# An attention block on one core: three Q or K products in one go, V behind the results, a written-out beginning and a new ending

## The reference

```
q, k, v = x @ Wq + bq, x @ Wk + bk, x @ Wv + bv          # 128x384 each, six heads of 64
s       = q_h @ k_h.T / sqrt(64) + where(adj, 0, -9e15)  # 128x128 for each head
p       = softmax(s)
ctx     = concat_h(p @ v_h)
y       = x + ctx @ Wf + bf
out     = (y - mean(y)) / sqrt(var(y) + 1e-5)
```

## Time and profile before

| what | value |
|---|---|
| median of three runs | 1030.92 us |
| the profiled execution's own time | 1031.09 us |
| its span, first to last instruction | 1029.3 us |
| TensorE busy | 1017.5 us, 99% |
| VectorE busy | 732.1 us, 71% |
| ScalarE busy | 596.4 us, 58% |
| GpSimd busy | 627.8 us, 61% |
| granted TensorE clock, mean | 0.999 |

### The profile page before, as it was taken

One profiled execution on the slowest core, in us unless ns is written; L12 is line 12 of the kernel. 1 busy time (PEld: TensorE's weight loads), 2 busy tenths in 40 slices (PEclk: granted clock), 3 DMA queues, 4 the chain that ended last, 5 costly groups with the idle time before them and its releaser, 6 DMA issues.

```text
span 1029.3 us, 26790 instructions
## 1 busy us (share of the span) xinstructions
PE 1017.5 (99%) x7185; PEld 906.5 (88%) x7185; DVE 732.1 (71%) x2822; ACT 596.4 (58%) x2127; POOL 627.8 (61%) x649
## 2 busy tenths in 40 slices
PE   8999999999999999999999999999999999999996
PEld 7889889889888898898888898888988988988886
DVE  3576777777677777767776776777777677767674
ACT  4565655656646656556556466465565565564563
POOL 1355666656665756656666566656566666666675
PEclk9999999999999999999999999999999999999999
DMA  7286676676666666766766766766667667666431
GB/s 197 77 209 183 174 192 159 177 193 164 181 183 168 189 177 171 195 166 173 193 161 175 192 162 185 186 166 190 172 172 196 165 176 184 166 176 183 146 122 62
DMA packets 337690, 176.48 MB, mean 171 GB/s; under 512 B 222336, under 2 KB 321792, under 8 KB 337664
## 3 DMA queue, kind: packets, MB, share of 16 engines
q1 hardware_dynamic: 336864, 175.79, 62.7%
q10 hardware_dynamic: 800, 0.39, 0.1%
HBM read 102.18 MB, written 73.92 MB: 171 GB/s over the span
## 4 chain that ended last, share of the span: by engine, by line
PE 98%; DVE 1%; issue 0%; ACT 0%; POOL 0%; POOLq 0%; DVEq 0%
PE qk_ps L379 14%; PE qk_ps L381 13%; PE qk_ps L380 13%; PE cov_ps L379 13%; PE cov_ps L381 13%; PE cov_ps L380 13%; PE scores_ps L395 9%; PE cov_ps L413 9%; PE qk_ps L475 0%; PE scores_ps L523 0%; DVE s_mask L606 0%; DVE xT_lo L595 0%; PE scores_ps L467 0%; PE scores_ps L483 0%; PE qk_ps L413 0%
## 5 line engine op out<-in xcount | busy, mean ns | idle before, releaser
L790 ACT ACTIVATE probs<-s_mask,neg_max 128x128 f32<-128x128 f32 x756 | 292.6, 390 | 4.3 <-DVE neg_max L612 4.3
L606 DVE CUSTOM_DVE_ANT_0 s_mask<-scores_ps,mask_bias 128x128 f32<-128x128 f32 x768 | 172.5, 287 | 89.8 <-PE scores_ps L395 85.9
L920 POOL TENSOR_TENSOR probs<-probs,inv_sum 128x768 f32<-128x768 f32 x126 | 186.0, 1477 | 78.2 <-DVE inv_sum L625 78.2
L915 POOL TENSOR_SCALAR y_sb<-y_sb,mean_var,rstd 128x384 f32<-128x384 f32 x124 | 205.2, 1655 | 22.8 <-POOL rstd L909 22.8
L618 DVE STREAM_TRANSPOSE p_turned<-probs 128x768 f32<-128x768 f32 x124 | 121.3, 978 | 113.3 <-POOL probs L920 113.3
L909 POOL TENSOR_TENSOR rstd<-var_eps,minus_half 128x1 f32<-128x1 f32 x128 | 72.5, 566 | 180.3 <-DVE var_eps L653 180.3
L807 ACT ACTIVATE qT<-qk_ps,bq_col 128x512 f32<-128x512 f32 x96 | 65.6, 683 | 155.4 <-PE qk_ps L381 155.4
L790 ACT ACTIVATION_READ_ACCUMULATOR probs<-s_mask,neg_max 128x1 f32 x756 | 142.7, 189 | 0.0
L595 DVE TENSOR_TENSOR xT_lo<-xT,xT_hi 128x384 fp32r<-128x384 f32 x120 | 113.2, 981 | 32.8 <-ACT xT_hi L775 32.6
L781 ACT CAST cT_hi<-cov_ps 128x384 fp32r<-128x384 f32 x126 | 60.5, 480 | 125.8 <-PE cov_ps L413 123.0
L798 ACT COPY v_sb<-cov_ps 128x384 f32<-128x384 f32 x124 | 59.5, 480 | 122.0 <-PE cov_ps L381 122.0
(11 more groups left out here) (76 smaller groups left out, 2007.4 us busy)
## 6 DMA issues: line engine op xcount, KB each, us to landing
p_out<-p_turned SPq DMA_DIRECT2D x124, 384.0 KB, 2.6
pT<-p_out SPq DMA_DIRECT2D x496, 96.0 KB, 2.4
x_in<-in_x SPq DMA_DIRECT2D x128, 192.0 KB, 3.5
out<-y_sb SPq DMA_DIRECT2D x128, 192.0 KB, 2.4
x_blocks<-in_x SPq DMA_DIRECT2D x360, 64.0 KB, 2.3
adj_u<-in_adj SPq DMA_DIRECT2D x32, 64.0 KB, 3.3
probs<-in_L_gnn_Wv SPq DMA_DIRECT2D x1, 576.0 KB, 6.2
pT<-in_L_gnn_Wf SPq DMA_DIRECT2D x1, 576.0 KB, 6.8
```

Of the source, the lines that this page charges most:

```text
L606: last = nc.vector.tensor_tensor_reduce(out=s_mask[:, e, h, :], in0=scores_ps[:, score_cols(e, h)], in1=mask_bias[:, e, :], scale=SCALE, s ...
L790: last = nc.scalar.activation(p_sb[:, e, h, :], s_mask[:, e, h, :], ACT.Exp, bias=neg_max[:, e, h:h + 1], scale=1.0, accum_out=row_sum[:, ...
L915: nc.gpsimd.tensor_scalar(y_sb[:, y, :], y_sb[:, y, :], mean_var[:, e, 0:1], rstd[:, e, 0:1], ALU.subtract, ALU.mult).then_inc(y_ready, 1)
L920: nc.gpsimd.tensor_tensor(p_sb[:, e, :, :], p_sb[:, e, :, :], inv_sum[:, e, :].unsqueeze(2).broadcast_to([P, HEADS, SEQ]), ALU.mult).then_ ...
```

## The change

Five things change.

- In every step the third Q/K job stands behind the first two, in front of the output products, and V follows directly on the output products.
- On VectorE a step's order behind `invert_sums(1)` is now: residual of graph 0, turn of graph 1, residual of graph 1, the two splits of x, then both statistics. Before it was: splits, both residuals, statistics 0, turn 1, statistics 1.
- The steps with p < 0 are replaced by a function `beginning` on each engine but GpSimd. V's weights are loaded by rows, and the first V product runs chunk by chunk as they come; four V products stand before the six Q/K jobs. 8 and 5 matmuls without use remain of 8, 7 and 12.
- The bias row is made by three VectorE instructions that scale Wf's rows by bv and add them, and one float32 matmul with ones, instead of three float32 matmuls.
- The ending: V of pairs 62 and 63 stands earlier on TensorE; the statistics and the scaling of pair 59, which belonged to step 61, move into the ending, on VectorE and GpSimd; pair 63 has its own slots for the statistics; graph 125 is scaled by GpSimd.

```diff
 # PE, step
-                for j in jobs[:2]:
+                for j in jobs:
                     qk_product(i, c, j)
...
                     for e in range(2):
                         out_product(c, p, e)
-                for j in jobs[2:]:
-                    qk_product(i, c, j)
                 if real(p + AHEAD, ENDING):
                     for e in range(2):
                         early_v(c, p, e)
 # PE, beginning
+            def beginning():
+                pe.wait_ge(ident_ready, 2)
+                warm_up(WARM_UPS[0])
+                transpose_x(0)
+                warm_up(WARM_UPS[1])
+                first_v()
+                transpose_x(2)
+                early_v(2, -2, 1)
+                transpose_x(3)
+                early_v(3, -1, 0)
+                early_v(3, -1, 1)
+                for j in range(NJ):
+                    qk_product(FIRST, AHEAD, j)
+                    if j in (1, 3):
+                        transpose_x(GROUP + j - 1)
+                        transpose_x(GROUP + j)
+                bias_product()
+            def first_v():
+                pe.wait_ge(xT_split, 1)
+                dst = cov_ps[0][:, 0:HID]
+                for k in range(KC):
+                    if k == KC - 1:
+                        transpose_x(1)
+                    x_hi, x_lo, v_hi, v_lo = v_operands(0)(k)
+                    pe.wait_ge(w_split["v"], k + 1)
+                    nc.tensor.matmul(dst, x_hi, v_hi, start=k == 0, stop=False)
+                    nc.tensor.matmul(dst, x_hi, v_lo, start=False, stop=False)
+                    last = nc.tensor.matmul(dst, x_lo, v_hi, start=False, stop=k == KC - 1)
 # PE, bias_product
-                pe.wait_ge(xT_split, GROUP + 1)
-                for k in range(KC):
-                    last = nc.tensor.matmul(xT_bank(0)[:, 0:HID], bv_wide[:, k, :], w_raw["f"][:, k, :],
-                                            start=k == 0, stop=k == KC - 1)
-                last.then_inc(bias_mm, 1)
+                pe.wait_ge(bv_scaled, KC)
+                pe.wait_ge(ones_ready, 1)
+                pe.wait_ge(v_copied, GROUP - 1)
+                nc.tensor.matmul(cov_ps[0][:, 0:HID], ones[:, :], bv_rows[:, KC - 1, :], start=True, stop=True
+                                 ).then_inc(bias_mm, 1)
 # DVE, step
-                if real(p + X_AHEAD, PAIRS):
-                    for e in range(2):
-                        split_x(c, e, 2 * (p + X_AHEAD) + e)
...
                 if real(p - LAG, PAIRS):
-                    for e in range(2):
-                        add_residual(i, c, e, 2 * (p - LAG) + e)
-                    find_stats(c, 0, 2 * (p - LAG))
+                    add_residual(i, c, 0, 2 * (p - LAG))
                 if real(p, PAIRS):
                     turn_blocks(i, c, 1, 2 * p + 1)
                 if real(p - LAG, PAIRS):
-                    find_stats(c, 1, 2 * (p - LAG) + 1)
+                    add_residual(i, c, 1, 2 * (p - LAG) + 1)
+                if real(p + X_AHEAD, PAIRS):
+                    for e in range(2):
+                        split_x(c, e, 2 * (p + X_AHEAD) + e)
+                if real(p - LAG, ENDING - 1 - LAG):
+                    for e in range(2):
+                        find_stats(c, e, 2 * (p - LAG) + e)
 # ACT, beginning: the other weights are issued behind the first rounding
+                round_x(FIRST, 0, 0, 0)
+                load_weight_part(act, "q", wq, 0)
+                load_weight_part(act, "q", wq, 1)
+                load_weight_part(act, "k", wk, 2)
+                round_x(FIRST, 0, 1, 1)
...
 # GpSimd, step (ENDING = 62, LAG = 2)
-                if real(p - LAG, PAIRS):
+                if real(p - LAG, ENDING - 1 - LAG):
                     for e in range(2):
                         normalise_y(c, e, 2 * (p - LAG) + e)
 # GpSimd, ending (a = 62, b = 63)
-                for e in range(2):
-                    add_bias(a // TURN, a % TURN, e, 2 * a + e)
-                normalise_probs(0, 2 * a)
-                normalise_probs(1, 2 * a + 1)
-                normalise_y(a % TURN, 0, 2 * (a - 2))
+                for e in range(2):
+                    normalise_probs(e, 2 * a + e)
+                normalise_y((a - 1) % TURN, 0, 2 * (a - 1 - LAG))
                 normalise_probs(0, 2 * b, last_probs)
-                normalise_y(a % TURN, 1, 2 * (a - 2) + 1)
+                normalise_y((a - 1) % TURN, 1, 2 * (a - 1 - LAG) + 1)
                 normalise_probs(1, 2 * b + 1, last_probs)
-                for e in range(2):
-                    add_bias(b // TURN, b % TURN, e, 2 * b + e)
-                for q in (a - 1, a, b):
+                for q in (a, b):
+                    for e in range(2):
+                        add_bias(q // TURN, q % TURN, e, 2 * q + e)
+                    for e in range(2):
+                        normalise_y(q % TURN, e, 2 * (q - LAG) + e)
+                for q in (a, b):
                     for e in range(2):
                         normalise_y((q + LAG) % TURN, e, 2 * q + e)
```

More of the change, by code:

```diff
@@ L79, in past, with run_steps @@
     eng.wait_ge(sem, value)
-def run_steps(eng, step, last, turns=PAIRS // TURN - 1):
-    for p in range(-X_AHEAD, TURN):
+def run_steps(eng, step, last, turns=PAIRS // TURN - 1, first=0):
+    for p in range(first, TURN):
         step(p // TURN, p % TURN)
@@ L164, in apart, with stats_slot @@
             eng.nop(nofuse=True)
+        def stats_slot(e, n):
+            return 2 + e if isinstance(n, int) and n >= BATCH - 2 else e
         def score_cols(e, h):
@@ L366, in ending @@
                         store_y(q, e)
-            run_steps(sp, step, ENDING, PAIRS // TURN - 2)
+            def beginning():
+                load_x(0, 0)
+                load_weight_rows(sp, "v", wv, 1)
+                for n in range(1, GROUP):
+                    load_x(n, n)
+                load_weight_part(sp, "k", wk, 0)
+                load_bias_column(sp, bq_col, bq, qk_biases_loaded)
+                load_bias_column(sp, bk_col, bk, qk_biases_loaded)
+                load_weight_part(sp, "k", wk, 1)
+                load_weight_part(sp, "q", wq, 2)
+                for n in range(GROUP, BY_MATMUL):
+                    load_x(n, n)
+                load_bias_column(sp, bv_col, bv, vf_biases_loaded)
+                sp.dma_start(bf_row[:, :], bf.rearrange("(a n) -> a n", a=1).broadcast_to([P, HID])
+                             ).then_inc(vf_biases_loaded, DMA)
+                sp.dma_start(w_raw["f"][:, :, :], wf.rearrange("(c p) n -> p c n", p=P)).then_inc(wf_loaded, DMA)
+            beginning()
+            run_steps(sp, step, ENDING, PAIRS // TURN - 2, -X_AHEAD)
             ending()
@@ L862, in ending @@
                     copy_pT(a, e)
-                exps(1, 2 * b + 1, last_probs)
-                for e in range(2):
-                    round_ctx(e, 2 * a + e)
                 for e in range(2):
@@ L869, in ending, with beginning @@
                     copy_pT(b, e)
-                for e in range(2):
-                    round_ctx(e, 2 * b + e)
+                for q in (a, b):
+                    for e in range(2):
+                        round_ctx(e, 2 * q + e)
+            def beginning():
+                round_x(FIRST, 0, 0, 0)
[3 more added lines that the diff above has]
+                round_x(FIRST, 0, 1, 1)
+                round_x(FIRST, 1, 0, 2)
+                copy_v(cov_ps[0], 0, 0)
+                round_x(FIRST, 1, 1, 3)
+                copy_v(cov_ps[1], 1, 1)
+                round_weight("q", 0)
+                round_weight("k", 0)
+                round_weight("q", 1)
+                round_weight("k", 1)
+                copy_v(cov_ps[0], 2, 2)
+                round_weight("k", 2)
+                copy_v(cov_ps[1], 3, 3)
+                round_weight("q", 2)
+                act.wait_ge(qk_biases_loaded, 2 * DMA)
+                copy_qk(FIRST, AHEAD, 0)
+                copy_qk(FIRST, AHEAD, 1)
+                for e in range(2):
+                    round_x(FIRST, 2, e, GROUP + e)
+                copy_qk(FIRST, AHEAD, 2)
+                copy_qk(FIRST, AHEAD, 3)
+                for e in range(2):
+                    round_x(FIRST, 3, e, GROUP + 2 + e)
+                copy_qk(FIRST, AHEAD, 4)
+                copy_qk(FIRST, AHEAD, 5)
+            beginning()
             run_steps(act, step, ENDING)
```

246 lines of the change are left out of this document (116 added, 130 removed).

## The result

The changed kernel takes 1024.64 us (median of 4 runs, 1023.86 to 1025.48), the kernel before 1030.67 in the same comparison: ratio 0.994, 95% interval 0.9924 to 0.9955. The forecast was 1026.8, faster with 0.77, range 1023.8 to 1030.2. The sign was right and the range held; the gain is 6.0 where 4.1 was forecast, and its parts are not where I had put them.

A forecast was written before the change was run, and what follows sets the result against it. TensorE, with 98% of the chain of waits, was taken to bound the kernel. Beginning -3.1, middle -1.2, ending +0.2 sum to -4.1: 1031.09 to 1027.0, less 0.17 for the median, 1026.8 us; range 1023.8 to 1030.2.

The forecast's parts named there:

- Third job, -0.02 a step: Middle, TensorE: third job directly behind the second runs without a wait, 0.02 us shorter; 60 steps, -1.2 us.
- V at no change: Middle, TensorE: V directly behind the output products costs 0, its residuals being done 0.8 and 0.75 us ahead.
- No wait for a residual: Middle, before V: both residuals end in time; the rival of a 0.1 us wait a step said 1032.6, chance 0.05.
- the ring shorter than a step by 0.6: Middle, chain through VectorE and GpSimd into the next step: 15.1 us against a step of 15.68, no cost.
- The rival of a ring that turns slower than TensorE: Middle, VectorE and GpSimd: ring of 15.9 us, 0.22 a step, +12.8 over 58 steps, 1040.9; chance 0.08.
- the pair of splits at 1.8: Middle, VectorE: x splits keeping their old 1.8 us by meeting GpSimd, where the forecast took 2 x 0.5.
- Beginning, -3.1: Start to scores of pair 0: at 28.8 us instead of 31.94, gain 3.1.
- the change of the clock at 6.3: Beginning, TensorE: rate goes from 1.2 to 2.4 GHz at about 6.3 us, V's first matmuls losing about 0.3.
- The rival of the late clock: Beginning, TensorE: V must bring up the clock itself and loses 2.3 us, 1029.1; chance 0.12.
- the gap before V: Beginning, TensorE: gap of 0.3 us between the last of the 5 matmuls and V, named as speaking for a late clock.
- Ending, -0.9 and +1.1: Scores of pair 62 come 0.9 us earlier, GpSimd's last power 1.1 later against them; +0.2 in all.
- the ending pays as well: Rival, ending: GpSimd is not last, -2.3 us and the +0.2 drops out, 1024.3; chance 0.15.

The follow-up runs named there:

- experiment 1: Changed kernel with TensorE's old order in the steps (two jobs, output products, third job, V); 1028.66 us, ratio to the kernel before 0.9981.
- experiment 3: Changed kernel with the third job between the two output products on TensorE; 1027.74 us.
- experiment 2: Changed kernel with VectorE's old order in the steps, TensorE's new order kept; 1026.29 us.
- experiment 4: Changed kernel with one 128x384 addition more on GpSimd in each step, behind the scaling of y; 1029.35 us.
- experiment 5: Changed kernel with two 128x384 additions more on GpSimd in each step, behind the scaling of y; 1075.21 us, ratio to the kernel before 1.0427.
- experiment 6: Changed kernel with four 128x384 additions more on GpSimd in each step, behind the scaling of probabilities, where nothing in the ring waits; 1025.32 us.
- experiment 7: Changed kernel with 11 and 6 matmuls without use in the beginning in place of 8 and 5; 1024.29 us.
- experiment 9: Changed kernel with GpSimd's x_bias of pairs 62 and 63 moved into idle time before its full stretch; 1021.75 us, ratio to the kernel before 0.991.

## Why the prediction was right, and where its parts were not

- *Third job, -0.02 a step.* Mis-sized. The term was bounded by 0 and -0.04, and I took the middle; it measured -0.044 (2.084 to 2.040), -2.5 in all. The row that bore on it was the one I had: 2.08 behind an output product and 2.04 behind a job. Step 1, at 2.13, was the worse witness, since a wait was mixed in. The end of the range was the better choice.
- *V at no change.* Mis-sized: -0.017 a step (3.232 to 3.215), -1.0 in all. In the earlier trace rows V was 3.24; in the 58 steps it lay between 3.22 and 3.25, which I had not read. V behind a job has a late chunk: in every step of experiment 1, where residual 0 ends 2.6 to 2.9 us before it, and in part of the steps of the kernel before, where mostly 0.20 to 0.30 us lie between. Together with the third job this makes -0.061 x 58 = -3.5 in place of -1.2. Experiments 1 and 3 show the neighbours as the cause. VectorE's order has a share (0.02 a step in V in experiment 2, where the residual is only just in time, but +0.006 on top of TensorE's old order, 15.674 to 15.680); how a residual that ends 0.2 to 0.3 before V changes the spacing in V is not explained.
- *No wait for a residual, the ring shorter than a step by 0.6.* Right: a ring of 14.88 (forecast 15.1), 0.73 in hand against a step of 15.61 (experiments 4 and 5). The rival of a ring that turns slower than TensorE needed 0.6 us more than I counted, and it would have taken 0.73 more than there is; the pair of splits at 1.8 would have been past it by 0.1 only, at 1.58 it isn't (experiment 6).
- *Beginning, -3.1.* The sum of the work was right: with an early clock scores of pair 0 come at 28.5 (forecast 28.8). The rate was wrong: what failed is the change of the clock at 6.3, with the loss of 0.3 that I counted for it: it came at about 10. The rival of the late clock said 2.3 for a first V at half rate; the profiled execution shows about 1.4 (29.93 against 28.52). I had named the gap before V as what speaks for it. The runs speak rather for the gap before the transposes (x of graph 0 landed at 3.90, 0.38 after TensorE was done with its 8 matmuls; in the kernel before, the transposes start at 3.50 without a wait that the view names), but one execution has that gap and an early clock, so the cause stays open. The Trainium skill (TensorE: Matmul & The Clock Gate, "Part 4: PE-mode transpose") would have it that transposes don't count for the clock; experiment 7 disagrees as the earlier trace rows did, since nothing but transposes, of the identity and of x, stood before a first product with use at full rate. (That these ran in the mode which the page means, no row shows.)
- *Ending, -0.9 and +1.1.* Right in mechanism: GpSimd is full and is the last link, the last power at S62+36.8. The wait of 0.78 before the scores of pair 62 went, but TensorE is busy 0.11 longer in these two steps (25.14 to 25.25), so 0.64. From there to the last power it was 36.2 and is 36.8, so +0.6 and not +1.1: I had taken the difference against my own working of before (35.8), where the trace gave 36.2. The tail behind the last power is 3.6 in both. The rival "the ending pays as well" did not happen in the change; experiment 9 takes work off GpSimd and makes the ending pay.
- *The range* held, and the time lay 2.2 below the forecast. The middle alone, the third job and V, gained 2.3 more than forecast and everything from the scores of pair 60 on 0.2 more, the beginning 1.1 less: that these misses partly cancel is luck. The rest is that the median is 0.84 under the profiled execution's time, where I had 0.17.

## What to carry to other kernels

A bound that a row gives twice (2.08 behind one neighbour, 2.04 behind another) is a measurement and not an end of a range: take it whole, and multiply it by the steps. Give a product that feels its neighbour the same neighbour in every step that repeats. Idle time of an engine does not mean room: find the ring in which it waits, and measure what the ring has in hand by putting work in; more than twice that work, put where nothing in the ring waits for it, cost nothing in a step of the middle here (in the short step 1 it cost 1 us). Where an engine is full towards the end, look for its work that depends on nothing late and move it into its last idle time.

## What the runs showed of the hardware that was not expected

- A float32r product with 512 columns behind one with 384 takes 2.08 in place of 2.04, all nine matmuls a little longer (0.231 for 0.227 from start to start), and one with 384 behind one with 512 has a late chunk of 0.55 for 0.52. No wait shows in the trace.
- TensorE's rate in the beginning changed from half to full at 5.2 to 6.5 us in the three executions with no gap before the transposes, and at 7.5 to 10 in eight of nine with one of 0.30 to 0.56 us; in the ninth, with a gap of 0.47, it changed at 5.3. The column of the granted clock showed 1.00 in each.
- Four GpSimd additions of 0.80 took 3.81 together beside VectorE's splits, which took 872 ns in the median in place of 550: the meeting costs both.
- A V that waits for its residual starts 0.15 us after the residual's end (experiment 5, in each step), so the 0.25 of experiment 2 is nearly a wait, though no view names one.
